# Two-layer cross-attention and feed-forward kernel: a new order of work in its first stage

## The reference

```
ifg   = concat(q, k, v)                  # q = layernorm(x), k = v = ctx
ig,fg = (ifg @ igate_w.T + igate_b).T, (ifg @ fgate_w.T + fgate_b).T
cs    = cumsum(log_sigmoid(fg))
log_D = where(tril, cs[:,:,None] - cs[:,None,:], -inf) + ig[:,None,:]
m     = max(log_D, -1);  D_mat = exp(log_D - m)
C     = (qh @ kh.T / sqrt(32)) * D_mat
norm  = max(|C.sum(-1)|, exp(-m))
h     = (C / (norm + 1e-6)) @ vh         # then a norm over the 256 features
x     = x + (h - mu) / sqrt(var + 1e-5) * ln_scale
```

## Time and profile before

| | us |
|---|---|
| runs | 562.52, 562.78, 564.67 |
| median | 562.78 |
| profiled execution, its own time | 560.74 |
| its span | 559.0 |
| TensorE busy | 538.2 (96%) |
| VectorE busy | 319.1 (57%) |
| ScalarE busy | 243.4 (44%) |
| GpSimd busy | 72.5 (13%) |

### The profile page before, as it was taken

How to read it: one execution, slowest core, us unless ns; L and a number is a source line. 1 busy time by engine, 2 the same in 40 slices (tenths; PEclk the granted TensorE clock), 3 DMA queues, 4 the chain that set the end, 5 groups by cost and what they waited for, 6 DMA issues and landing times.

```text
span 559.0 us, 8453 instructions
## 1 busy us (share of the span) xinstructions
PE 538.2 (96%) x2773; PEld 451.8 (81%) x2773; DVE 319.1 (57%) x776; ACT 243.4 (44%) x456; POOL 72.5 (13%) x116
## 2 busy tenths in 40 slices
PE   7899898999999999999999999999999999999996
PEld 5677777888998888778888788889788889788886
DVE  6678788868777689652443543434542543633333
ACT  6446657758798633551122441122541122631111
POOL 5232443204210441000000000000000000000000
PEclk9999999999999999999999999999999999999999
DMA  6693636356958776000000000000000000000001
GB/s 174 195 262 113 163 85 173 94 215 203 403 166 278 259 241 204 0 1 1 0 2 9 28 2 1 0 1 21 18 0 1 0 1 33 6 1 0 1 0 40
DMA packets 29860, 47.44 MB, mean 85 GB/s; under 512 B 3392, under 2 KB 21184, under 8 KB 29440
## 3 DMA queue, kind: packets, MB, share of 16 engines
q1 hardware_dynamic: 24848, 30.14, 17.1%
q0 software_dynamic: 4848, 16.78, 9.4%
q10 hardware_dynamic: 128, 0.05, 0.0%
HBM read 40.27 MB, written 2.10 MB: 76 GB/s over the span
## 4 chain that ended last, share of the span: by engine, by line
PE 59%; issue 8%; POOL 2%; DVE 1%; POOLq 0%; DVEq 0%
PE ps L953 58%; POOL rstd L457 1%; POOL h L575 1%; PE ps L609 0%; PE ps L917 0%; DVE qr L1595 0%; DVE x L1583 0%; DVE xn L1345 0%; DVE alT L1622 0%; DVE xT L1352 0%; POOL w L564 0%; POOLq L575 0%; POOL w L566 0%; PE ps L908 0%; DVE ot L1675 0%
## 5 line engine op out<-in xcount | busy, mean ns | idle before, releaser
L1308 ACT ACTIVATE h<-ps,scol 128x512 f32<-128x512 f32 x64 | 44.2, 690 | 175.3 <-PE ps L953 175.2
L953 PE MATMUL ps<-hBt,h 128*128 128x512 f32 x512 | 117.5, 390 | 0.0
L953 PE MATMUL ps<-hA,h 128*128 128x512 f32 x512 | 117.3, 390 | 0.0
L953 PEld LDWEIGHTS ps<-hA,h 128*128 128x128 f32 x512 | 95.9, 188 | 20.4 <-DVE hA L1649 0.6
L953 PEld LDWEIGHTS ps<-hBt,h 128*128 128x128 f32 x512 | 95.8, 188 | 20.3 <-DVE hBt L1649 0.6
L953 PE MATMUL ps<-xT,w 128*128 128x512 f32 x256 | 61.7, 396 | 1.0 <-DVE xT L1352 1.0
L953 PEld LDWEIGHTS ps<-xT,w 128*128 128x128 f32 x256 | 46.1, 188 | 14.9 <-issue 6.0
L1667 DVE CAST hBt<-h 128x512 fp32r<-128x512 f32 x32 | 13.7, 427 | 73.7 <-ACT h L1308 73.7
L1667 DVE CAST hA<-h 128x512 fp32r<-128x512 f32 x32 | 13.7, 427 | 70.0 <-ACT h L1308 70.0
L457 POOL TENSOR_TENSOR rstd<-ve,mhalf 128x4 f32<-128x4 f32 x16 | 16.4, 1028 | 263.1 <-DVE ve L1340 263.1
L1291 ACT ACTIVATE silD<-ps,scol 128x512 f32<-128x512 f32 x32 | 22.1, 689 | 45.1 <-PE ps L953 45.1
(11 more groups left out here) (180 smaller groups left out, 881.7 us busy)
## 6 DMA issues: line engine op xcount, KB each, us to landing
looked<-w_all_in SPq DMA_DIRECT2D x16, 704.0 KB, 5.9
h<-w_all_in POOLq DMA_DIRECT2D x16, 512.0 KB, 6.9
V<-ctx_in SPq DMA_DIRECT2D x8, 512.0 KB, 4.8
Qb<-xT SPq DMA_DIRECT2D x64, 64.0 KB, 2.0
w<-w_all_in POOLq DMA_DIRECT2D x3, 1024.0 KB, 7.0
x<-x_in SPq DMA_DIRECT2D x4, 512.0 KB, 4.7
kstA<-ctxT_in SPq DMA_DIRECT2D x4, 512.0 KB, 4.8
kstC<-ctxT_in SPq DMA_DIRECT2D x4, 512.0 KB, 6.9
```

The costliest lines, as they stand in the source:

```text
L953: last = mm(o, a, b, start=(k == 0 and p == 0), stop=(k == n_k - 1 and p == 1))
L1308: fn(h32[:, m % 2, :], ps[:, 2 + m % 4, :], ACT.Gelu, scale=scol[:, L + 1, m:m + 1])\
```

## The change

The edit has these parts, all in stage A.

- SyncE: the loads of x for groups 2 and 3 go out at the start, ahead of the second key load, not behind the queries of quarter 0. In the loop the queries of quarter 2 are ahead of the key load, and the values behind the queries of quarter 3.
- GpSimd and VectorE: the low half of the keys is made in two passes (one for each 128 of the 256 features), and a new semaphore `klo_first` tells of the first; `gates` waits for each part by itself.
- GpSimd: the mean and the roots for the norm of x, and the root for the group's first batch, are ahead of the wait for the gate rows and the weight pieces, not behind them.
- TensorE: `turn_e` comes behind the last qk of quarter 3, not ahead of its exponents.
- VectorE: the head norm of the group's first batch moves from quarter 2 to behind both weighs of quarter 3, and the floor copy from quarter 2 to between these two weighs.

```diff
@@ SyncE, start
             sp.dma_start(diag[:, :], diag_in).then_inc(s["consts"], 16)
+            for g in range(2, G):
+                sp.dma_start(x[:, Q * g:Q * g + Q, :], x_in[Q * g:Q * g + Q].rearrange("b s d -> s b d"))\
+                    .then_inc(s["x_rest"], 16)
             sp.wait_ge(s["klo_done"], 1)
...
             queries_in(0, 0, 0)
-            for g in range(2, G):
-                sp.dma_start(x[:, Q * g:Q * g + Q, :], x_in[Q * g:Q * g + Q].rearrange("b s d -> s b d"))\
-                    .then_inc(s["x_rest"], 16)
@@ SyncE, loop
+                    queries_in(g, u, 2)
                     with sp.If(i < 1):
 
                         sp.wait_ge(s["klo_done"], 2 + u)
                         sp.dma_start(kstA[:, :, :], ctxT_in[:, :, (2 + u) * GT:(3 + u) * GT])\
                             .then_inc(ctxT_ld[u], 16)
-                    queries_in(g, u, 2)
-                    def early():
+                    if u == 0:
                         gates_in(gn)
+                    else:
+                        with sp.If(i < 1):
+                            gates_in(gn)
+                    queries_in(g, u, 3)
+                    def following():
                         sp.wait_ge(s["pv_done"], Q * g + 2)
                         values(gn, 1 - u)
+                        lead_in(gn, 1 - u)
...
@@ GpSimd
+            def k_lo_apart(n, u):
+
+                pool.wait_ge(s["khi_done"], n + 1)
+                for c, name in ((0, "klo_first"), (1, "klo_done")):
+                    nc.gpsimd.tensor_tensor(kT[:, u, 1, c, :], kstA[:, c, :], kT[:, u, 0, c, :], ALU.subtract)\
+                        .then_inc(s[name], 1)
...
+                    pool.wait_ge(s["mv_ready"], g + 3)
+                    nc.gpsimd.tensor_tensor(nmean[:, :], mv[:, :, 0], mone[:, :], ALU.mult)\
+                        .then_inc(s["nmean_ready"], 1)
+                    inv_root(g + 2)
...
+                    h_root(Q * g, 0)
                     if u == 0:
                         pool.wait_ge(s["gate_moved"], 32 * (g + 2))
                         pool.sem_inc(s["pieces_go"], 1)
@@ TensorE
                     if c == KD:
+                        pe.wait_ge(s["klo_first"], g + 1)
+                    if c == KD + 1:
                         pe.wait_ge(s["klo_done"], g + 1)
...
-                        if q == Q - 1:
-                            more(lambda: turn_e(gn))
-                            if u == 1:
-                                if_later(pe, i, flag_total)
+                        if q == Q - 1 and u == 1:
+                            if_later(pe, i, flag_total)
                         for k in (2 * q, 2 * q + 1):
                             expo(g, u, k)
                         for k in (2 * q, 2 * q + 1):
                             qk(g, u, k)
+                        if q == Q - 1:
+                            more(lambda: turn_e(gn))
@@ VectorE
+                        if q == Q - 1:
+                            more(lambda: floor_copy(gn, 1 - u))
                         weigh(g, 2 * q + 1)
...
                         if q == 2:
                             finish(b - 1, u, q - 1)
-                            more(lambda: floor_copy(gn, 1 - u))
-                            head_norm(b - 2, q - 2)
                         if q == Q - 1:
+                            head_norm(b - 3, 0)
                             finish(b - 1, u, q - 1)
```

More of the change, by code:

```diff
@@ L238, in two_layers @@
             raw_here raw_seen hnm_ready hve_ready lns_ready gw_lo gw_cast const_set mv_ready rstd_ready nmean_ready shift_ready xn_ready tr_done xhi_done xlo_done x_free
-            khi_done klo_done gate_done gate_copied gate_moved ab_ready ln_ready ncs_ready er_ready z_ready
+            khi_done klo_done klo_first gate_done gate_copied gate_moved ab_ready ln_ready ncs_ready er_ready z_ready
             z_moved er_turned et_ready expo_done d_ready qk_done c_ready pv_done pv_used hstat_ready hrs_ready
@@ L350, in _ @@
                             .then_inc(ctxT_ld[u], 16)
-                    queries_in(g, u, 2)
-                    def early():
+                    if u == 0:
                         gates_in(gn)
+                    else:
[3 more added lines that the diff above has]
+                    def following():
                         sp.wait_ge(s["pv_done"], Q * g + 2)
                         values(gn, 1 - u)
+                        lead_in(gn, 1 - u)
                     if u == 0:
-                        early()
+                        following()
                     else:
                         with sp.If(i < 1):
[L360 to L366, removed]
+                            following()
             sp.wait_ge(s["expo_done"], UN * G)
@@ L519, in _ @@
                         with pool.If(i > 0):
-                            k_lo(G - 1, kstA[:, :, :], 1)
+                            k_lo_apart(G - 1, 1)
                             h_root(2 * Q - 1, 1)
@@ L523, in _ @@
                         with pool.If(i < 1):
-                            k_lo(2, kstA[:, :, :], 0)
+                            k_lo_apart(2, 0)
                         h_root(Q * g - 1, 1)
+                    pool.wait_ge(s["mv_ready"], g + 3)
+                    nc.gpsimd.tensor_tensor(nmean[:, :], mv[:, :, 0], mone[:, :], ALU.mult)\
+                        .then_inc(s["nmean_ready"], 1)
+                    inv_root(g + 2)
+                    pool.wait_ge(s["nmean_ready"], g + 1)
+                    pool.wait_ge(s["rstd_ready"], g + 3)
+                    nc.gpsimd.tensor_tensor(shift[:, :], nmean[:, :], rstd[:, :], ALU.mult)\
+                        .then_inc(s["shift_ready"], 1)
+                    h_root(Q * g, 0)
                     if u == 0:
@@ L534, in _ @@
                             pieces(1, 0)
[L535 to L543, removed]
                     if u == 0:
@@ L1356, in k_lo @@
                 dve.wait_ge(s["khi_done"], n + 1)
-                v.tensor_tensor(kT[:, par, 1, :, :], kstA[:, :, :], kT[:, par, 0, :, :], ALU.subtract)\
-                    .then_inc(s["klo_done"], 1)
+                for c, name in ((0, "klo_first"), (1, "klo_done")):
+                    v.tensor_tensor(kT[:, par, 1, c, :], kstA[:, c, :], kT[:, par, 0, c, :], ALU.subtract)\
+                        .then_inc(s[name], 1)
             def gate_a(g):
```

## The result

The changed kernel takes 566.13 us (median of 7 runs, 565.52 to 567.32), the one before 562.78 in the same comparison (7 runs, 561.42 to 564.67); the ratio is 1.0066 [1.0040, 1.0092]. The forecast was 560.8, with a range of 558.6 to 564.2. The profiled execution took 567.32, with a span of 565.6 against 559.0.

A forecast was written before the change was run, and what follows sets the result against it. SyncE's queue, from zp through row moves and quarter 0's queries to the next group's first qk, was taken to set the pace, not TensorE. x -1.2, keys -1.2, GpSimd +0.4 gave -2.0 us: median 560.8, range 558.6 to 564.2.

The forecast's parts named there:

- GpSimd: statistics and h_root ahead of the weight pieces: Groups 0 to 2: later pieces delay quarter 0's queries, landings 8.05 us in all against 7.63, so +0.4 us.
- zp to the last move's start: Loop from VectorE's zp to the start of SyncE's last quarter 0 query move: 4.86, 4.70 and 4.83 us.
- the row moves behind zp: Sign: the prediction is wrong if zp is later against its group's first qk than 15.6 us.
- the times from the last move of quarter 0's queries to the first qk: Sign, groups 1 to 3: the prediction is wrong if these three landings sum to more than 10 us.
- The clock: TensorE's granted clock: 1.00, the 2.4 GHz level, in the stretches shown; the edit gives no reason for another.
- Rival C: Qb of quarter 0 in each new group: queries collide with pieces on the DMA engines, +3.9 us, 566.7; chance 0.12.
- x at the start: Start of stage A: row moves land without the x loads' traffic, first exponent -1.2 us, bounds -1.8 to -0.3.
- Keys in two passes: GpSimd's low half of the keys: TensorE's wait of 1.15 us shrinks, -1.2 us, bounds 0.5 to 1.3.
- turn_e: TensorE, loop: waits for Er go, worth nothing beyond 0.34 us at the second boundary.
- The wait at qk 7: TensorE, quarter 3: qk 7 is late next, waiting for the weigh that reads its bank; under 1 us.
- SyncE's order: SyncE's loop: quarter 2's queries arrive sooner, but no step of the sum hangs on them; nothing.

The follow-up runs named there:

- the filler: Changed kernel with 13 useless matmuls of 128x512 added on TensorE between the causal part and the exponents of groups 1 and 3; 561.72 us, ratio 0.9998.
- the pieces later still: Changed kernel with GpSimd's weight pieces waiting for the next group's four row moves to have landed, not for its gate rows; 569.28 us, ratio 1.0119.
- SyncE's loop order put back: Changed kernel with GpSimd's order and SyncE's loop order of before, x of groups 2 and 3 still loaded at the start; 560.67 us, ratio 0.9940.

## Why the prediction was wrong

**The step that failed is "GpSimd: statistics and h_root ahead of the weight pieces".** I had the pieces' new time in group 0 about right (37.9 forecast for the first issue, 38.72 measured; last landing forecast for 46.0, seen at 47.4). In groups 1 and 2, which I took as alike, they were further off: 17.03 and 15.29 us behind the group's first qk instead of 11.30 and 11.80 before. I asked only what it does to the move that had been late before, the queries of quarter 0. I priced that at +0.4. The row moves are issued in the same microseconds as the pieces, ahead of the queries and needed ahead of them, by the exponents. In my sum they stood in the term "zp to the last move's start", taken as fixed at 4.86 us: true of the issue, not of the landing. The exponents' wait is a second branch of the loop that the sum lacked. By the ratios the step costs 4.6 us in waits and 3.8 in clock, 8.4 in all (1.0066 against 0.9917), where I had +0.4. Two of the signs that I had named show it: the row moves behind zp went out 17.93 us behind the first qk of group 1, not 15.6, and the times from the last move of quarter 0's queries to the first qk sum to about 11.4 us, more than 10.

**The clock was no term at all.** I wrote that the edit gives no reason for another. Behind waits of 3.40 and 2.57 us it fell, and the sum should have held, for each such wait that a rival makes, a chance of some busy time behind it at the 1.2 GHz level. Rival C would have come to more than 566.7 with it; the run in which the wait was at C's place took 569.28.

**Rival C** had the sign, about the size (566.7 against 566.13) and the wrong move: its place was Qb of quarter 0, where the changed kernel does not wait. Its agreement in size is chance, since it had nothing for the clock. The rule of the Trainium skill behind it (DMA: Bandwidth & Descriptors, Queues, rings and completion order) agrees with these traces: the exponents that wait for rows of 16 KB start between 0.1 us ahead of the last piece's landing and 0.7 behind it, in groups 1, 2 and 3 of the changed kernel (47.63, 72.76 and 97.40 against 47.4, 72.1 and 97.1), and in group 1 with GpSimd's order alone (47.91 against 48.0), with the filler (47.22 against 47.3) and with GpSimd's order put back (44.44 against 43.8). Whether it is this order of completion or only the shared bandwidth that holds the rows back, no run here tells apart. I held the rule against the queries and not against the rows. The same page, section Issuing engines are not separate DMA queues, says that transfers share the same engines whichever engine starts them; the waits in three places of three kernels agree.

**x at the start: right at the first exponent, but worth more.** -1.2 forecast; 1.14 at the first exponent, but 2.8 at stage B in the traces, 1.9 by the medians and 2.8 by the ratios. The sum had no term for the gate rows and the pieces that come later with the late loads.

**Keys in two passes: right in kind, too large.** -1.2 forecast; 0.5 by the medians, 1.5 by the ratios, neither told from zero, and with the keys whole the wait is only 0.67. By the traces it is the smaller figure: from the first exponent to stage B are 83.41 us with the keys whole and 82.94 with two passes. What had taken the rest of the 1.15 before is not shown.

**turn_e: nearly right.** Nothing forecast (0.34 at most); 0.7 by the medians, 1.4 by the ratios, within the spread. That 3.5 us of idle TensorE can be worth that little supports the reading by a sum of steps, and not by idle time. The wait at qk 7 that I named as next is there, 0.67 at most (0.74 with GpSimd's order put back).

**SyncE's order: priced at nothing, worth about 1.3** (0.2% by the ratios, not told from zero), because of quarter 3's queries. In the kernel before TensorE waited only 0.29 us there, behind its wait for Er. That the moved turn uncovered this wait and SyncE's new order covers it again is argued from the traces; no kernel had just these two put back.

**Without GpSimd's part** my terms give -2.4, and the profiled execution of that kernel is 2.5 below that of before; the medians differ by 3.6, and by the ratio it is 4.7. With x worth more than its term and the keys less, the agreement of the traces is in part luck. That version, 557.81, beats both kernels and is the one to keep; with only the root put back (558.39) the time is not told from it.

## What to carry to other kernels

When a burst of large transfers is moved, list every small move that is issued from its first issue to its last landing (here some 9 us) and who waits for each, not only the move that was late before. Then compare the burst's last landing with the time at which the first of them is needed: in the kernel before the row moves went out in the middle of the burst and cost nothing, since it had landed at 43.7 and TensorE came at 44.94. A few microseconds later put the wait on the rows, and a few more put it on the queries and made it longer. And a wait of TensorE of some microseconds is to be priced twice: itself, and the stretch at half clock that may follow.

## What was not expected of the hardware

The clock's fall is short and counts for much: with 3.40 us of idling came some 7 us at 0.50, with 2.57 us some 3.4. The length of one wait does not decide it: in the profiled executions it fell with waits of 4.48, 3.40, 3.32, 3.10, 2.57, 2.06 and 1.47 us, and stayed at 1.00 with others of 2.89, 2.34, 1.84 and 1.78. The profiled execution with GpSimd's new order alone had no fall, while nine others of the same kernel had a lower mean.

It also goes with most of the scatter of the kernel before. In the set beside "the pieces later still" and "SyncE's loop order put back", its seven executions with a mean clock of 0.999 or 1.000 took 560.77 to 561.50 us, the six at 0.994 to 0.996 took 563.06 to 564.04, and the four at 0.988 to 0.993 took 564.73 to 566.93. The profiled execution on which my sum was made (560.74, clock 0.999) was one without such a fall; what divides it from the median of 562.78 is of the size of one fall, so it is probably not part of the work. The mean clock alone does not tell: one execution with GpSimd's order put back had a mean of 0.970 and took 557.88 us, like the others.
